# Two layers of attention with experts: where attention results are multiplied by reciprocals, where one norm is applied, and how narrow heads are grouped

## The reference

```python
# layer 0: causal attention, heads of 8
x = layernorm(x + attention0(x))      # softmax(q k' / sqrt(8)), lower triangle, times v
x = layernorm(x + experts0(x))        # relu, top 2 of 8
# layer 1: causal attention of low rank, heads of 8
x = layernorm(x + attention1(x))      # the norm called k = 3 in the kernel
# then a third attention that is not causal, with only 4 numbers per head, in front of the experts
scores = einsum(Q[..., :4], K) / sqrt(4)
ao = einsum(softmax(scores), V)       # 16 heads x 4
moe = experts1(ao @ o_w + o_b)        # gelu, top 2 of 8
x = layernorm(x + x + 0.3 * moe)
```

## Time and profile before

| | us |
|---|---|
| median of 3 runs | 1165.69 (1164.51 to 1167.61) |
| the profiled execution | 1166.3 |
| its span (first to last instruction) | 1164.6 |
| TensorE busy | 1077.7 (93%) |
| VectorE busy | 883.9 (76%) |
| ScalarE busy | 764.9 (66%) |
| GpSimd busy | 305.0 (26%) |

### The profile page before, as it was taken

The page is one execution under the profiler, slowest core; times in us unless marked ns, Lnnn a source line. Parts: engine busy times, 40 slices in busy tenths (PEclk is TensorE's granted clock), DMA queues, the critical chain, the costliest instruction groups (busy, mean ns, idle before and its releaser), DMA issues. The chain is left out here.

```text
span 1164.6 us, 24392 instructions
## 1 busy us (share of the span) xinstructions
PE 1077.7 (93%) x8338; PEld 569.1 (49%) x8338; DVE 883.9 (76%) x2563; ACT 764.9 (66%) x1527; POOL 305.0 (26%) x843
## 2 busy tenths in 40 slices
PE   8999999989999988999999998898889898899997
PEld 5465665656767655666655532221122221137775
DVE  6999989882433497889978899799999899804435
ACT  4576776766444446777776677888888688875443
POOL 4234433231115225433346211230110100100001
PEclk9899999999999999999999999999999999999999
DMA  7355431100001601344222221002111000000000
GB/s 200 75 121 156 104 84 33 43 23 2 1 1 38 157 22 33 96 106 103 66 75 56 55 38 25 18 18 45 26 36 38 11 18 13 6 1 1 10 10 19
DMA packets 39563, 57.62 MB, mean 49 GB/s; under 512 B 9408, under 2 KB 14992, under 8 KB 39056
## 3 DMA queue, kind: packets, MB, share of 16 engines
q1 hardware_dynamic: 39440, 56.06, 19.6%
HBM read 30.81 MB, written 24.64 MB: 48 GB/s over the span
## 5 line engine op out<-in xcount | busy, mean ns | idle before, releaser
L911 ACT ACTIVATE probs<-bank 128x512 f32<-128x512 f32 x1088 | 575.9, 601 | 214.8 <-PE bank L1346 213.6
L1027 DVE TENSOR_REDUCE tile_max<-bank 128x1 f32<-128x512 f32 x768 | 495.5, 683 | 55.6 <-PE bank L1332 53.2
L1332 PE MATMUL bank<-qk 125*128 125x512 bf16 (+1 forms) x1280 | 387.2, 356 | 54.9 <-DVE tile_max L1027 41.3
L1346 PE MATMUL bank<-qk 128*128 128x128 bf16 (+1 forms) x1664 | 384.6, 309 | 5.9 <-ACT probs L911 5.5
L1375 PE MATMUL bank<-probs,v_head 128*32 128x512 f32 (+3 forms) x3328 | 304.1, 454 | 0.1
L1332 PEld LDWEIGHTS bank<-qk 125*128 125x128 bf16 (+1 forms) x1280 | 105.4, 96 | 333.1 <-DVE tile_max L1027 225.4
L1023 DVE CUSTOM_DVE_ANT_0 bank<-bank,future 128x512 f32<-128x512 f32 (+3 forms) x512 | 243.5, 506 | 22.2 <-PE bank L1332 22.1
L1187 DVE SCALAR_TENSOR_TENSOR acc<-bank,gate,acc 128x128 f32<-128x128 f32 x248 | 69.7, 343 | 158.4 <-PE bank L1501 158.4
L1346 PEld LDWEIGHTS bank<-qk 128*128 128x128 bf16 (+1 forms) x1664 | 138.2, 97 | 68.1 <-ACT probs L911 22.0
L1375 PEld LDWEIGHTS bank<-probs,v_head 128*32 128x32 f32 x3328 | 139.7, 109 | 53.4 <-issue 30.5
L931 ACT ACTIVATE probs<-bank,sb_b 128x512 f32<-128x512 f32 x128 | 81.0, 684 | 123.1 <-PE bank L1489 123.1
(11 more groups left out here) (148 smaller groups left out, 648.9 us busy)
## 6 DMA issues: line engine op xcount, KB each, us to landing
qk<-qk_parts SPq DMA_DIRECT2D x160, 144.0 KB
qk_parts<-q_parts SPq DMA_DIRECT2D x48, 192.0 KB, 2.4
qk_parts<-k_parts SPq DMA_DIRECT2D x48, 192.0 KB, 2.9
qk_parts<-q_parts SPq DMA_DIRECT2D x24, 96.0 KB, 2.3
qk_parts<-k_parts SPq DMA_DIRECT2D x24, 96.0 KB, 2.9
sb_w<-in_w SPq DMA_DIRECT2D x8, 256.0 KB, 3.7
sb_w<-in_w SPq DMA_DIRECT2D x2, 1024.0 KB, 5.9
qk<-neg_rows SPq DMA_DIRECT2D x96, 6.0 KB
```

Of the source, the lines that this page charges most:

```text
L911: nc.scalar.activation(probs[:, hd.probs_place(c), :], S2[i % len(S2)][:], ACT.Exp, scale=hd.a.scale).then_inc(sem("probs"), 1)
L1027: ins = nc.vector.tensor_reduce(largest, s1[:, at:at + P * count], AX.X, ALU.max)
L1332: ins = mm(s1[:, at:at + P * count], qk[hd.query_rows, hd.place, 0, P * t:P * (t + 1)], qk[hd.query_rows, hd.place, 1, P * k0:P * (k0 + co ...
L1346: ins = mm(s2[:, at:at + P * count], qk[hd.key_rows, hd.place, 1, P * j:P * (j + 1)], qk[hd.key_rows, hd.place, 0, P * q0:P * (q0 + count) ...
```

## The change

The narrow heads of a sequence form three groups, of 6, 5 and 5 heads, where they formed four of 4. Their values lie in six slots, by the place in the group. The multiplication of results by reciprocals goes from VectorE to GpSimd, for all heads: VectorE takes the reciprocal at the same place as before (`inverse`), and GpSimd multiplies (`normalise`) in the second batch of the same head, after the second mask and before the steps of the table. The norm k = 3 of chunks 2 and 3 goes from ScalarE to GpSimd as tensor_scalar with two scalars from memory; the table is unchanged. Other norms stay with ScalarE.

```diff
-        self.groups = (3, 3, 3, 3, 2, 2) if causal else (4, 4, 4, 4)
+        self.groups = (3, 3, 3, 3, 2, 2) if causal else (6, 5, 5)
...
-        self.v_slot = self.at_in_group + 3 * (group % 2) if self.a.causal else self.slot
+        self.v_slot = self.at_in_group + (3 * (group % 2) if self.a.causal else 0)
...
+def by_gpsimd(k, c):
+    return k == 3 and c >= CB
+NORMS_OF = {by: [step[1:] for step in NORMS if by_gpsimd(*step[1:]) == by] for by in (False, True)}
...
-        v_heads = [sb("v_head8", [P, 6, TB, Q]), sb("v_head4", [P, RING, TB, Q])]
+        v_heads = [sb("v_head8", [P, 6, TB, Q]), sb("v_head4", [P, 6, TB, Q])]
...
+        def normed(eng, k, c):
+            by = by_gpsimd(k, c)
+            eng.wait_ge(sem("normed_gpsimd" if by else "normed"), NORMS_OF[by].index((k, c)) + 1)
...
# GpSimd, steps of the table
+                    if kind == "norm" and by_gpsimd(*which):
+                        k, c = which
+                        pool.wait_ge(sem("rstd"), ROOT_OF[(k, c)])
+                        for t in range(TPC * c, TPC * (c + 1)):
+                            ins = nc.gpsimd.tensor_scalar(x[:, t, :], x_plus[:, t, :], rstd[:, t:t + 1], shift[:, t:t + 1],
+                                                          ALU.mult, ALU.add)
+                        ins.then_inc(sem("normed_gpsimd"), 1)
...
# GpSimd, add_quarters
-                ge(pool, "normalised", 2 * (i - 1))
+                ge(pool, "normalised", i - 1)
...
# GpSimd
+            def normalise(i):
+                first = GROUPS[i][0]
+                a, G, h = first.a, len(GROUPS[i]), first.h
+                o = total[:, i % 2, :, 0:G * a.dv].rearrange("p t (g d) -> p t g d", g=G)
+                pool.wait_ge(sem("inverse"), i + 1)
+                nc.gpsimd.tensor_tensor(
+                    a_tok[:, of_sequence(first.b), a.hd * h:a.hd * (h + G)].rearrange("p t (g d) -> p t g d", g=G),
+                    o[:, :, :, 1:a.dv], den_inv[:, i % 2, :, 0:G].unsqueeze(3).to_broadcast([P, TB, G, a.hd]),
+                    ALU.mult).then_inc(sem("normalised"), 1)
...
                     if k == 1 and hd.a.causal:
                         mask(g, 1)
+                    if k == 1 and g - 2 >= run.start and HEADS[g - 2].ends_group:
+                        normalise(GROUP[g - 2])
...
                 add_quarters(GROUP[run.stop - 1])
+                normalise(GROUP[run.stop - 1])
...
# ScalarE
-                    if kind == "norm":
+                    if kind == "norm" and not by_gpsimd(*which):
...
# VectorE
-            def normalise(i):
+            def inverse(i):
...
                 dve.wait_ge(sem("total"), ADDS[i + 1])
-                nc.vector.reciprocal(den_inv[:, i % 2, :, 0:G], o[:, :, :, 0]).then_inc(sem("normalised"), 1)
-                dve.wait_ge(sem("normalised"), 2 * i + 1)
-                nc.vector.tensor_tensor(
-                    a_tok[:, of_sequence(first.b), a.hd * h:a.hd * (h + G)].rearrange("p t (g d) -> p t g d", g=G),
-                    o[:, :, :, 1:a.dv], den_inv[:, i % 2, :, 0:G].unsqueeze(3).to_broadcast([P, TB, G, a.hd]),
-                    ALU.mult).then_inc(sem("normalised"), 1)
+                ge(dve, "normalised", i - 1)
+                nc.vector.reciprocal(den_inv[:, i % 2, :, 0:G], o[:, :, :, 0]).then_inc(sem("inverse"), 1)
```

More of the change, by code:

```diff
@@ L326 @@
 ROOT_OF = {(step[1], c): i + 1 for i, step in enumerate(ROOTS) for c in step[2]}
-NORM_OF = {step[1:]: i + 1 for i, step in enumerate(NORMS)}
 STATS = [step for place in PLACES for step in BETWEEN[place] if step[0] == "stats"]
@@ L361, in build @@
         v_all = [sb("v8", [P, NH, TB, 9]), sb("v4", [P, NH, TB, 5])]
-        v_heads = [sb("v_head8", [P, 6, TB, Q]), sb("v_head4", [P, RING, TB, Q])]
+        v_heads = [sb("v_head8", [P, 6, TB, Q]), sb("v_head4", [P, 6, TB, Q])]
         probs = sb("probs", [P, 9, CH])
         sums = sb("sums", [P, 2, CH])
-        by_quarter = sb("by_quarter", [P, 2, 4, 4, 27])
+        by_quarter = sb("by_quarter", [P, 2, 4, 4, 30])
         pairs = sb("pairs", [P, 4, 27])
-        total = sb("total", [P, 2, TB, 27])
+        total = sb("total", [P, 2, TB, 30])
         tile_max = sb("tile_max", [P, RING, TB, 2])
@@ L372, in build @@
         neg_rows = sb("neg_rows", [PARTS * TB, RING, P], BF16)
-        den_inv = sb("den_inv", [P, 2, TB, 4])
+        den_inv = sb("den_inv", [P, 2, TB, 6])
         a_tok = sb("a_tok", [P, NT, D])
@@ L602, in _ @@
             for c in range(NCH - 1):
-                sp.wait_ge(sem("normed"), NORM_OF[(4, c)])
+                normed(sp, 4, c)
                 store_out(tiles(c))
@@ L664, in between @@
                             loaded(pool, "attn1")
-                            pool.wait_ge(sem("normed"), NORM_OF[(2, c)])
+                            normed(pool, 2, c)
                         nc.gpsimd.tensor_tensor(x_plus[:, tiles(c), :], x[:, tiles(c), :],
@@ L1034, in find_max @@
                                             negate=True).then_inc(sem("neg_max"), 1)
-            def normalise(i):
+            def inverse(i):
                 first = GROUPS[i][0]
-                a, G, h = first.a, len(GROUPS[i]), first.h
+                a, G = first.a, len(GROUPS[i])
                 o = total[:, i % 2, :, 0:G * a.dv].rearrange("p t (g d) -> p t g d", g=G)
                 dve.wait_ge(sem("total"), ADDS[i + 1])
-                nc.vector.reciprocal(den_inv[:, i % 2, :, 0:G], o[:, :, :, 0]).then_inc(sem("normalised"), 1)
-                dve.wait_ge(sem("normalised"), 2 * i + 1)
-                nc.vector.tensor_tensor(
-                    a_tok[:, of_sequence(first.b), a.hd * h:a.hd * (h + G)].rearrange("p t (g d) -> p t g d", g=G),
-                    o[:, :, :, 1:a.dv], den_inv[:, i % 2, :, 0:G].unsqueeze(3).to_broadcast([P, TB, G, a.hd]),
-                    ALU.mult).then_inc(sem("normalised"), 1)
+                ge(dve, "normalised", i - 1)
+                nc.vector.reciprocal(den_inv[:, i % 2, :, 0:G], o[:, :, :, 0]).then_inc(sem("inverse"), 1)
             def head(run, g, found):
@@ L1059, in head @@
                     if k == 0 and g - 2 >= run.start and HEADS[g - 2].ends_group:
-                        normalise(GROUP[g - 2])
+                        inverse(GROUP[g - 2])
                 return found
@@ L1191, in experts @@
                     if m == 0:
-                        normalise(last)
+                        inverse(last)
                     between(at_unit(f, m, 1))
@@ L1396, in between @@
                         groups_done = GROUP[L * NH + H * (c // CB + 1)]
-                        pe.wait_ge(sem("normalised"), 2 * groups_done)
+                        pe.wait_ge(sem("normalised"), groups_done)
                         move_in("taken", TAKEN[step])
@@ L1418, in between @@
                         k, c = which
-                        pe.wait_ge(sem("normed"), NORM_OF[(k, c)])
+                        normed(pe, k, c)
                         move_in("taken", TAKEN[step])
```

## The result

The changed kernel takes 1153.96 us (1153.23 to 1155.2, four runs) against 1165.35 (1164.51 to 1167.61) for the kernel before in the same session: ratio 0.990, 95% interval 0.9883 to 0.9918. Measured again among the experiments it was 1154.66 against 1166.54, 0.9895 (0.9872 to 0.9917). Forecast: 1154.9, with 1150.5 to 1161 around it. The profiled execution took 1155.2, its span 1153.5, which is 11.1 less than before.

A forecast was written before the change was run, and what follows sets the result against it. It took TensorE to bound causal heads and experts, VectorE narrow heads. Causal -4.7 and narrow -6.1 us made -10.8: 1155.5 for the profiled execution of 1166.3, 1154.9 beside the median; range 1150.5 to 1161 for 8 in 10.

The forecast's parts named there:

- Part 1: Causal heads: with the multiply off VectorE, TensorE's stalls shrink, 5.0 us gained (bounds 0 and 8.8).
- rival A: Causal stages give nothing back, another wait lying just behind: 6.1 us gained in all, 1159.6; chance 0.12.
- Part 2: GpSimd's multiply takes 0.6 us (bounds 0.2 and 1.3), hidden; 0.3 us charged where GpSimd also splits queries and keys.
- rival D: Slower: GpSimd sets the causal pace from 3.1 us per multiply; at 4.0 us the total is 1176.5; chance 0.05.
- Parts 3 and 4: Narrow heads: no multiply on VectorE, 2.8 us gained; two group boundaries fewer per layer, 0.7 gained.
- part 6: Head 70: sums meet value and key projections, 0.3 us lost; head 86: TensorE waits for the gate, 1.5 lost.
- Part 5: Head 68: norms off ScalarE and boundary gone, ending TensorE's stall and half clock; 4.4 us gained (bounds 2 and 4.9).
- Rival B: Head 86's gate wait drops the clock, costing 4.5 us, and head 68 keeps 2.2 of stall: 1160.1; chance 0.12.
- The sum: Whole kernel: causal -4.7 and narrow -6.1 us, total -10.8; 1155.5 for the profiled execution, 1154.9 beside the median.
- Rival C: Whole kernel: no change, within 0.3% or 3.5 us, A and B both; 1164 us; chance 0.07.

The follow-up runs named there:

- the whole first set of experiments: Kernel before with only the multiply, groups or norms changed, and changed kernel with norms back on ScalarE: 1157.83, 1165.41, 1163.17 and 1156.77 us.
- Gate first: Changed kernel with GpSimd doing the gate before the addition of quarters in a head's second batch: 1152.60 us, ratio 0.9874 to the kernel before.

## Why the prediction was right

The time fell well inside the range, and each mechanism was where it had been put. That the total came within 1 us is partly luck, as the last point says. By its own steps:

- **Part 1, the multiply off VectorE: right, a little small.** A three-head group gave 0.34 instead of 0.26, a two-head group 0.22 instead of 0.17 (four such heads, where five had been counted), and heads 20, 26 and 52 gave 0.44 to 0.56, where the largest ordinary term was 0.40. The step was "the smaller of the freed time and TensorE's stall", read from the idle time shown; the heads gained 0.08 and 0.05 more. In the three-head one idle time fell by 0.20 and busy time by 0.14 (7.34 to 7.20), so it seems that part of the stall had stood in the profile as busy time, and that idle time understates what can be won. TensorE's waits for VectorE fell to 8.0 us, not to the 7 forecast, though the heads gained more. Head 7, beside the addition of the earlier trace rows, gave 1.01 instead of 0.8. Nothing new came behind the old wait, so rival A is out.
- **Part 2, GpSimd multiplies: right.** 0.53 us for 192 numbers (0.6 taken from the earlier trace rows), 0.42 for 128, and no new wait; the 0.3 charged for heads with splits of queries and keys does not show. Three times the work changes almost nothing, six times makes rival D true.
- **Parts 3 and 4: right, 0.8 and 0.4 too small.** The stage at VectorE's pace gave about 3.6 for 2.8 and 0.8 for 0.4. A boundary costs 0.71 us where it arrives (heads 70, 75, 91) and gives 0.70 or 0.71 where it leaves (72, 88). In head 70 that is all, so the collision that part 6 had put at 0.3 there does not show.
- **Part 5, head 68: right in size (4.6 for 4.4), incomplete in cause.** It took the norms and the boundary as one. Apart they are worth 3.9 and 2.65, so each covers part of the other. Its 4.9 us of VectorE's idle time in four waits came from a window that runs 2.7 us beyond the head; in the head itself it is 4.7 in three. GpSimd's norms take 3.48 us for eight (0.45 each, 0.3 taken), inside the bounds and hidden, since TensorE wants x only two batches later.
- **Part 6: right.** TensorE waits 1.13 us for the gate (1.5 forecast), the head costs 1.60 (1.5), and the clock does not fall further. Gate first removes at least 1.0 of it. Rival B is out.
- **The sum** was 10.8 for an execution; the two profiled ones differ by 11.1, but only because 2.2 at the start hides part of 13.3, and the second profile of the changed kernel gives 11.5 head by head. The terms were too small by 0.7 to 2.5 us in all, and the clock and the start vary by as much from one execution to the next. That the result lies 1 us from the forecast is partly luck. Rival C is out, since the interval of the ratio ends at 0.9918.

The medians of the parts add up to 9.0 + 1.4 + 3.7 = 14.1 us, the whole gives 11.9. The intervals of the parts (3 us either way for the multiply) are too wide for this difference of 2.2. The traces show an overlap more plainly: in the narrow heads the three parts give 11.4 us one by one and 7.4 together. Of these 4.0, 2.0 lie in head 68, 0.8 in head 86 and 1.2 in the rest, partly because the multiplies of the two boundaries that vanish are counted twice.

## What to carry to other kernels

Where a second engine runs close behind the first (here 88% busy beside 96%), look first at the idle time of the first that stands right behind the second one's extra instruction: it is a first estimate of what moving the instruction can return, and here the heads gave back a little more. Price the engine that receives the work by its slack before the next thing that someone waits for, and test that slack by issuing the work several times: one was free and three almost, six cost more than the change had won. In heads 36, 68 and 85 a stall was followed by 3.4 to 6.8 us at 1.2 GHz and so was paid a second time. A block that holds one engine for some microseconds (a routing, a split, a norm in front of a copy) is therefore worth cutting into pieces or moving even if the work stays the same.

## What the runs showed of the hardware

**VectorE beside GpSimd.** The kernel with the groups alone repeats: VectorE's multiply of 192 numbers beside GpSimd's addition of 512.

```profile
91.53 0.98 DVE L1043 TENSOR_TENSOR a_tok<-total,den_inv 128x192 f32<-128x192 f32 x1
```

```profile
91.02 1.27 POOL L666 TENSOR_TENSOR x_plus<-x,sb_bo 128x512 f32<-128x512 f32 x1
```

It takes 0.98 us there and 0.36 alone. Here and in the earlier trace rows it ends 0.21 to 0.22 us after the addition does, with starts 0.51 and 0.46 us behind the addition's: it looks like waiting for the addition's end, not like running slower. In the changed kernel the reciprocal at 90.86, which reads one tensor, stands beside the same addition and takes its usual 0.30. The GpSimd addition itself stays at 1.27 to 1.28. The Trainium skill (GPSIMD Engine Reference, Specifications) says that VectorE instructions with two SBUF inputs contend with GpSimd for shared SBUF interfaces; the traces agree.

**Stretches at half clock come and go.** The same program had one from 460.9 to 464.3 us in one execution and from 456.8 to 463.6 in another. Other versions had one near 658, 664, 676, 709 or 897 us, in heads whose code was the same, and each cost 0.6 to 1.6 us. Head 86 took 14.0 to 14.9 us in six traces with the same code for it. With one profile for each kernel, a difference of 1 to 1.5 us in a single head is no evidence unless the clock column is read with it.

**The start.** The first four projections of two profiles, of before and of the changed kernel; the code is the same:

```profile
6.13 1.98 PE L1292 MATMUL bank<-xT,sb_wqT 128*128 128x512 f32 x4 [0.69 <-ACT xT L798]
```

```profile
6.47 3.78 PE L1318 MATMUL bank<-xT,sb_wqT 128*128 128x512 f32 x4 [0.69 <-ACT xT L828]
```

1.98 against 3.78 us is about half the rate, though the clock column reads 1.00 in both. That reading is empty: the trace of the changed kernel has no record of the clock before 10.3 us, just where the slow projections end, and that of the kernel before has none before 5.0. The second profile of the changed kernel has 1.98. The first negated maximum ended at 30.6 to 31.5 us in eight traces and at 33.4 to 33.6 in five. The five are the first profile of the changed kernel and the whole first set of experiments; in all five the projections take 3.73 to 3.78 us and the first record of the clock comes at 10.0 to 10.3 us, in the eight 1.98 or 1.99 and 4.7 to 6.2. So the late start goes with TensorE at half its rate until 10 us. It does not follow the kernel; whether it follows the chip, since each set had its own, can't be told from one set each. What sets it is open. A comparison of two spans should start behind it.
